# Register addresses of eight loaded offsets worked out at the load, three to an instruction, in a graph attention + MoE kernel

## What is computed

```python
h = jnp.einsum('ni,hid->nhd', layernorm(x), W)            # 4 heads of 64
e = (h[src] * a_src).sum(-1) + (h[dst] * a_dst).sum(-1)   # a score for each edge and head
e = jnp.where(e > 0, e, 0.2 * e)
alpha = jnp.exp(jnp.minimum(e - segment_max(e, dst)[dst], 20.0))
alpha = alpha / (segment_sum(alpha, dst)[dst] + 1e-08)
x = x + segment_sum(alpha[:, :, None] * h[src], dst).reshape(N, 256) @ W_out
t = layernorm(x)
probs = softmax(t @ router_w.T); rw, re = top_k(probs, 2); rw = rw / rw.sum(-1)
x = x + t + sum(combine[:, e] * (gelu(t @ w1[e] + b1[e]) @ w2[e] + b2[e]) for e in range(8))
```

## Time and profile before

| | before |
|---|---|
| median of three runs | 1516.63 us |
| time of the profiled execution | 1515.7 us |
| its span, first to last instruction | 1513.6 us |
| mean granted TensorE clock | 0.953 |
| TensorE matmuls busy | 1381.5 us (91%) |
| VectorE, ScalarE, GpSimd busy | 1108.2 (73%), 985.0 (65%), 840.0 us (55%) |

### The profile page before, as it was taken

The page is one execution under the profiler, slowest core; times in us unless marked ns, Lnnn a source line. Parts: engine busy times, 40 slices in busy tenths (PEclk is TensorE's granted clock), DMA queues, the critical chain, the costliest instruction groups (busy, mean ns, idle before and its releaser), DMA issues.

```text
span 1513.6 us, 28779 instructions
## 1 busy us (share of the span) xinstructions
PE 1381.5 (91%) x7177; PEld 1120.8 (74%) x7177; DVE 1108.2 (73%) x3057; ACT 985.0 (65%) x2522; POOL 840.0 (55%) x886
## 2 busy tenths in 40 slices
PE   5925775899999999999999999999999999999998
PEld 4723443688888888788878787878787878787887
DVE  6726775778787878787878787878777878777543
ACT  3713664567777767676767676767676767777732
POOL 1347777666666666666666665656565656661000
PEclk9965786699999999999999999999999999999999
DMA  9564654434444444444444444444444343464000
GB/s 223 145 196 121 191 148 118 134 102 122 112 122 113 121 113 120 115 118 118 120 113 120 116 114 119 117 118 111 123 109 128 104 132 99 134 89 66 1 18 18
DMA packets 89817, 174.79 MB, mean 115 GB/s; under 512 B 22471, under 2 KB 56081, under 8 KB 89625
## 3 DMA queue, kind: packets, MB, share of 16 engines
q0 software_dynamic: 40448, 111.89, 29.5%
q1 hardware_dynamic: 48103, 60.78, 13.2%
q10 hardware_dynamic: 1106, 0.27, 0.1%
HBM read 159.26 MB, written 14.43 MB: 115 GB/s over the span
## 4 chain that ended last, share of the span: by engine, by line
PE 65%; issue 8%; ACT 7%; DVE 6%; POOL 5%; ACTq 2%; DMA 1%; DVEq 0%; POOLq 0%
PE agg_ps L1148 22%; PE ob L1223 17%; PE hb L1177 14%; POOL ring L747 5%; PE kbank L1110 3%; PE ob L1259 3%; DVE ring L855 2%; ACT acc L1377 2%; PE ob L1229 2%; ACT agg_ps L1380 2%; ACTq L660 1%; PE kbank L1125 1%; ACT L1391 1%; PE kbank L1124 1%; ACT hT L1409 1%
## 5 line engine op out<-in xcount | busy, mean ns | idle before, releaser
L747 POOL DMA_INDIRECT ring<-table,srcE x832 | 808.0, 971 | 476.6 <-PE agg_ps L1148 237.5
L1148 PE MATMUL agg_ps<-ring,oh 128*128 128x260 f32 x1664 | 552.5, 425 | 19.1 <-ACT agg_ps L1380 15.7
L1377 ACT COPY acc<-agg_ps x831 | 306.7, 369 | 182.4 <-PE agg_ps L1148 109.4
L1223 PE MATMUL ob<-w_sb,hT 128*125 128x256 f32 x1600 | 408.7, 381 | 1.7
L1380 ACT COPY agg_ps<-zc 128x260 f32 x832 | 314.7, 378 | 98.7 <-ACT acc L1377 3.2
L1148 PEld LDWEIGHTS agg_ps<-ring,oh 128*128 128x128 f32 x1664 | 291.7, 199 | 79.6 <-issue 41.8
L1223 PEld LDWEIGHTS ob<-w_sb,hT 128*125 128x125 f32 x1600 | 295.8, 188 | 53.1 <-issue 9.2
L855 DVE TENSOR_TENSOR ring<-ring,kbank 128x1024 f32<-128x1024 f32 x208 | 244.9, 1215 | 51.9 <-ACT ring L1399 51.5
L1409 ACT ACTIVATE hT<-hb,b_sb 128x375 f32<-128x375 f32 (+1 forms) x272 | 153.7, 565 | 122.8 <-PE hb L1177 121.9
L992 DVE SCALAR_TENSOR_TENSOR y<-ob,cmb,y 125x256 f32<-125x256 f32 x400 | 189.2, 476 | 45.1 <-PE ob L1223 41.7
L1177 PE MATMUL hb<-xTh,w1l 128*128 128x376 f32 (+1 forms) x544 | 186.7, 424 | 0.0
(11 more groups left out here) (280 smaller groups left out, 1340.6 us busy)
## 6 DMA issues: line engine op xcount, KB each, us to landing
OT<-relb_d SPq DMA_DIRECT2D x52, 512.0 KB
ring<-table,srcE POOLq DMA_INDIRECT x832
y<-in_x_dram SPq DMA_DIRECT2D x50, 125.0 KB
out_dram<-y SPq DMA_DIRECT2D x50, 125.0 KB
table<-hrow SPq DMA_DIRECT2D x25, 227.5 KB
acc<-in_x_dram SPq DMA_DIRECT2D x2, 1568.0 KB
acc<-in_L_ffn_w_dram SPq DMA_DIRECT2D x1, 2048.0 KB, 11.9
w_sb<-in_L_ffn_w_dram SPq DMA_DIRECT2D x1, 2048.0 KB, 11.8
```

Of the source, the lines that this page charges most:

```text
L747: pool.indirect_dma_start(out=rings[b % RING][:, k, :], out_offset=None, in_=table[:, :], in_offset=bass.IndirectOffsetOnAxis(ap=srcE[:, t ...
L1148: T.matmul(aggf[:, bass.ds(bank_of[k // 8][k % 8], ROW)], oh[:, (4 * b + q) % OHQ, k % 4, :], rings[b % RING][:, k, :], start=False, stop= ...
L1223: t = T.matmul(o[0:Q, 0:D], hT[:, e % 2, f, cols], w2_sb[:, e, f, :], start=f == 0, stop=f == KC - 1)
L1377: A.copy(accf[:, bass.ds(row_of[h][k % 8], ROW)], aggf[:, bass.ds(closed[h][k % 8], ROW)]).then_inc(S["ev"], 1)
```

## The change

A new helper `worked_out(eng, views)` asks for the addresses of a list of views of one engine. It is called right behind each `loads` that brings table offsets, with the eight views that will be used (one on VectorE), and the matmuls and copies take the finished views. The compiler puts the work for eight addresses into three register instructions. Nothing else is edited, and the matmuls, copies and loads of TensorE and ScalarE keep their order.

```diff
--- before.py
+++ after.py
@@ -660,6 +660,10 @@
                 return nc.values_load_multi_w_load_instructions(ap, engines=[eng], min_val=0, max_val=top_,
                                                                 skip_runtime_bounds_check_because=WHY)[1]
 
+            def worked_out(eng, views):
+                for a in views:
+                    eng.lower_ap(a)
+
             FETCHED = 16 * 4
             fetched = lambda b: FETCHED * (b // RING + 1)
             HC = lambda g, e, f: 2 * NE * g + 2 * e + f + 1
@@ -838,13 +842,15 @@
                     first = {}
 
                     def bank_of_first(b):
-                        first["at"] = loads(ENG.DVE, tabs[0:1, b % 3, 0, 0:4], (AB - 1) * 512)[0]
+                        at = loads(ENG.DVE, tabs[0:1, b % 3, 0, 0:4], (AB - 1) * 512)[0]
+                        first["at"] = aggf[:, bass.ds(at, ROW)].rearrange("p (h w) -> p h w", h=H)
+                        worked_out(v, [first["at"]])
 
                     def rescale(b):
                         dve.wait_ge(S["sc"], b + 1)
                         dve.wait_ge(S["agg"], BT * b)
                         dve.wait_ge(S["zr"], BT * b - 1)
-                        a = aggf[:, bass.ds(first["at"], ROW)].rearrange("p (h w) -> p h w", h=H)
+                        a = first["at"]
                         v.tensor_tensor(a, a, sc[:, :].unsqueeze(2).to_broadcast([P, H, HW]), ALU.mult).then_inc(S["rs"], 1)
 
                     def message(b, q):
@@ -1097,7 +1103,9 @@
                     def blocks_of_tiles(b, half):
 
                         pe.wait_ge(fld[b % RING], fetched(b))
-                        block_of[half] = loads(ENG.PE, tabs[0:1, b % 3, 2, 8 * half:8 * half + 8], (NB - 1) * 3 * H)
+                        rows_ = loads(ENG.PE, tabs[0:1, b % 3, 2, 8 * half:8 * half + 8], (NB - 1) * 3 * H)
+                        block_of[half] = [d3[:, bass.ds(r, 3 * H)] for r in rows_]
+                        worked_out(T, block_of[half])
 
                     def d_of_edges(b, half):
                         if half == 0:
@@ -1107,7 +1115,7 @@
                                 pe.wait_ge(S["otc"], 1)
                         for j in range(8):
                             t = 8 * half + j
-                            m = T.matmul(D_ps[:, t * 3 * H:(t + 1) * 3 * H], OT[:, t * P:(t + 1) * P], d3[:, bass.ds(block_of[half][j], 3 * H)],
+                            m = T.matmul(D_ps[:, t * 3 * H:(t + 1) * 3 * H], OT[:, t * P:(t + 1) * P], block_of[half][j],
                                          start=True, stop=True)
                         if half == 1:
                             m.then_inc(S["D"], 1)
@@ -1130,7 +1138,9 @@
                     def banks_of_tiles(b, h):
 
                         pe.wait_ge(fld[b % RING], fetched(b))
-                        bank_of[h] = loads(ENG.PE, tabs[0:1, b % 3, 0, 8 * h:8 * h + 8], (AB - 1) * 512)
+                        at = loads(ENG.PE, tabs[0:1, b % 3, 0, 8 * h:8 * h + 8], (AB - 1) * 512)
+                        bank_of[h] = [aggf[:, bass.ds(r, ROW)] for r in at]
+                        worked_out(T, bank_of[h])
 
                     def aggregate(b, k):
                         t, q = b * BT + k, k // 4
@@ -1145,7 +1155,7 @@
                             pe.wait_ge(S["am"], 1)
                         elif t > 1:
                             pe.wait_ge(S["zr"], t - 1)
-                        T.matmul(aggf[:, bass.ds(bank_of[k // 8][k % 8], ROW)], oh[:, (4 * b + q) % OHQ, k % 4, :], rings[b % RING][:, k, :],
+                        T.matmul(bank_of[k // 8][k % 8], oh[:, (4 * b + q) % OHQ, k % 4, :], rings[b % RING][:, k, :],
                                  start=False, stop=True, skip_group_check=True).then_inc(S["agg"], 1)
 
                     def ahead(it, k):
@@ -1359,11 +1369,17 @@
                         if k == 11:
                             act.wait_ge(fld[b % RING], fetched(b))
                         if k in (5, 11):
-                            row_of[h] = loads(ENG.Activation, tabs[0:1, b % 3, 3, part], (NB - 1) * ROW)
+                            at = loads(ENG.Activation, tabs[0:1, b % 3, 3, part], (NB - 1) * ROW)
+                            row_of[h] = [accf[:, bass.ds(r, ROW)] for r in at]
+                            worked_out(A, row_of[h])
                         elif k in (3, 13):
-                            coming[h] = loads(ENG.Activation, tabs[0:1, b % 3, 1, part], (AB - 1) * 512)
+                            at = loads(ENG.Activation, tabs[0:1, b % 3, 1, part], (AB - 1) * 512)
+                            coming[h] = [aggf[:, bass.ds(r, ROW)] for r in at]
+                            worked_out(A, coming[h])
                         elif k in (7, 15):
-                            closed[h] = loads(ENG.Activation, tabs[0:1, b % 3, 4, part], (AB - 1) * 512)
+                            at = loads(ENG.Activation, tabs[0:1, b % 3, 4, part], (AB - 1) * 512)
+                            closed[h] = [aggf[:, bass.ds(r, ROW)] for r in at]
+                            worked_out(A, closed[h])
 
                     def evacuate(b, k):
 
@@ -1374,10 +1390,10 @@
                             act.wait_ge(S["agg"], t)
                             if t > 1:
                                 act.wait_ge(S["ev"], t - 1)
-                            A.copy(accf[:, bass.ds(row_of[h][k % 8], ROW)], aggf[:, bass.ds(closed[h][k % 8], ROW)]).then_inc(S["ev"], 1)
+                            A.copy(row_of[h][k % 8], closed[h][k % 8]).then_inc(S["ev"], 1)
                             act.wait_ge(S["ev"], t)
                             act.wait_ge(S["zr"], t)
-                        A.copy(aggf[:, bass.ds(coming[h][k % 8], ROW)], zc[:, 0:1].to_broadcast([P, ROW])).then_inc(S["zr"], 1)
+                        A.copy(coming[h][k % 8], zc[:, 0:1].to_broadcast([P, ROW])).then_inc(S["zr"], 1)
 
                     def evacuate_last():
                         act.wait_ge(S["agg"], NTS)
```

## The result

| | before | after |
|---|---|---|
| median | 1516.72 us (4 runs, 1516.58 to 1517.98) | 1478.93 us (4 runs, 1478.28 to 1479.79) |
| ratio | | 0.9749, 95% interval 0.9733 to 0.9766 |
| time of the profiled execution, and its span | 1515.7, 1513.6 us | 1478.9, 1476.0 us |
| mean granted TensorE clock | 0.953 | 0.955 |

The change saves 37.8 us. The forecast was 1482, the range 1467 to 1503.

The account below looks back on a forecast made before the run. TensorE, busy 196.5 of 200 us, was taken to set the pace. Savings of 35.5 and 2 us less 1 and 3 given back make 33.5, so 1515.7 becomes 1482.2, forecast 1482, range 1467 to 1503.

Parts of the forecast that it names:

- Score matmuls: TensorE's 16 score matmuls a batch: without register instructions between them, 35.5 us saved, between 29.5 and 39 us.
- Waits behind which an address stood: TensorE's aggregations that wait for a bank's clearing, 25 times: 0.08 us less each, 2 us saved, between nothing and 3.
- Three instructions behind each load: TensorE's 208 loads: 0.4 us more of sequencer each, mostly hidden by queued matmuls; 1 us lost at loads with less cover.
- ScalarE, put at nothing: ScalarE's two copies of a tile and its loads: relieved by some 60 us, but nothing of that shortens the kernel by itself.
- What grows back: TensorE's waits for ScalarE and VectorE grow as batches get shorter: 3 us given back, between none and 15.7.
- A register-addressed matmul that is itself slow for the sequencer: Rival, score matmuls: the register address itself slows the matmul, so only 29 us are saved, 1490 us; chance 0.14.
- The engine that takes back what TensorE saves: Rival: waits for VectorE's bursts and ScalarE's table loads take half of TensorE's saved time, 17 us left, 1499; chance 0.17.
- The slower rival: Rival: ScalarE's longer loads, 1.8 us a batch, reach TensorE through the clearing; at 60% the kernel takes 1538 us; chance 0.07.

Follow-up runs that it names:

- Scores alone: Only the addresses of the 16 score matmuls of a batch worked out at their loads, the rest as in the kernel before: 1493.31 against 1516.53 us, ratio 0.9853.

## Why the prediction was right

The time was within 3.1 us of the forecast, but two of its terms were wrong by 10 us and more, in opposite directions.

1. *Score matmuls, 35.5 us.* Right. The groups of eight fell from 62.1 to 25.4 us, 36.7 us; "both groups should take what the shortest one takes" is what the timeline shows (0.20 and 0.21 us). The busy time of the line fell by 29.3 us, near the lower bound of 29.5 that the prediction took from it: idle gaps of a starved group aren't in it.
2. *Waits behind which an address stood, 2 us.* Mis-sized: four aggregations and the transposes of xn are 16 us nearer to what stands before them. The price of one instruction was not the error: where the aggregation waits, its least distance behind the end of the clearing fell from 130 to 52 ns, 0.08 us as predicted. The count was: the prediction counted the 25 waits that the view of waits shows as idle, and an aggregation that is held up while the matmul before it still counts as busy isn't among them. ScalarE's share of it failed by the next point.
3. *Three instructions behind each load.* They take 74, 74 and 60 ns on TensorE, estimated at 61, and start 133 ns apart; from the end of the load to the end of the third it is 0.39 us, predicted 0.4. Nearly all are hidden, as said: from batch 4 on the next matmul of the program starts at least 0.77 us behind a load's end. The 1 us put down for the others is about what shows: behind the last load of batches 1, 2 and 3 tile 15's aggregation starts 0.44 us after the load's end, where it was 0.19. Even with the cover taken away a group lost only 0.26 us. That the waits now stand at the matmuls adds nothing to this cover. In the changed kernel none of the 203 loads of batches 0 to 51 starts before the end of the clearing that the aggregation ahead of it waits for. The closest 12 start 50 or 51 ns behind that end, some of them up to 1.5 us ahead of the aggregation itself. Before, the closest started 152 ns behind it. So the wait still holds a load that stands behind it; only the address instruction behind the wait is gone. That the sequencer "passes" the wait for `oh` at a score group is shown by no run. The term of the score matmuls doesn't need it: the groups take 0.20 and 0.21 us once their first matmul has started.
4. *ScalarE, put at nothing.* This step failed. "Nothing of that shortens the kernel by itself" was argued from ScalarE's waits for TensorE, 74 us. But these are a sum over all tiles; at k = 15, 12 and 6 it is TensorE that waits for ScalarE. In the kernel before, the aggregation stands there at its least distance behind the end of the clearing two tiles back (130 ns, within 5; 236 ns at k = 12, which also waits for `oh`) in 30, 15 and 12 of 45 batches. The two banks of lead are used up in these, and each clearing that comes 0.08 us sooner lets the aggregation two tiles on go sooner. Alone it is worth 10.3 us (1506.24). The idle time by its own issue grew as predicted in kind, from 0.44 us a time to 0.56 (99.9 us, 179 times), predicted 0.7, and cost nothing.
5. *What grows back, 3 us.* Mis-sized: 14.4 us. Of these 7.0 are the transpose of cmb, 4.0 that of eC and 3.4 the expert output. Scores alone bring back 10.4 of it. Ahead of the two transposes it is waits for VectorE, whose chains have a length of their own: where TensorE arrives sooner it waits. For the expert output no wait for VectorE of that size shows; its weight loads stand idle by their own issue for 11.6 us instead of 8.8, and the cause is open. The prediction took these from the sum of the waits of before, which says nothing of how close the others were behind.

Steps 2, 4 and 5 nearly cancel, 16 against 14.4, where the sum had 2 against 3 and 1. So the forecast's 1482 owes its nearness in part to chance. The lower bound of the range needed ScalarE's relief, and that came.

*The rivals.* A register-addressed matmul that is itself slow for the sequencer is refuted: eight of them without an instruction between take 0.20 us, each starting 25 ns behind the one before (median of 728 distances in the trace of the changed kernel). The engine that takes back what TensorE saves was partly true: 14.4 us, not half of the gain. ScalarE's table loads, which that rival names, are 101 of 1.28 us each before and after. On the slower chip the larger part of the gain is missing, but what took it isn't shown. The slower rival is refuted by the kernel with ScalarE's edit alone, which is faster.

## What to carry to other kernels

In this kernel an address from a register cost TensorE's sequencer some 0.12 us with its short matmul. Between short matmuls it showed: 36.7 us over 102 groups of eight. Between matmuls of 0.4 us next to nothing did: beside the other two parts, taking the 832 of the aggregation away was worth 1.2 us in the account. So look for runs of short instructions, not for the line with most instructions. Get all addresses of such a run out of it; whether they stand at the load or right ahead of the run, joined or single, made no difference here. A wait summed over all tiles in one direction (ScalarE for TensorE) doesn't mean that the other direction is slack: sort distances between starts by the place in the loop before an edit is put at nothing.

## What the runs showed of the hardware

- In the trace of the kernel before, the sequencers' rows hold one register instruction for each matmul or copy with such an offset: 832 for the score matmuls and 832 for the aggregations (37 ns each), 831 for the closing copies (55 ns) and 832 for the clearings (43 ns). Taken in order, each of these 1664 matmuls has its first weight load at least 48 ns behind the end of its own, and each of the 1663 copies starts at least 41 ns behind it. They also keep the waits: of the 830 aggregations that wait for a clearing, none has its register instruction start before the end of that clearing, and the closest starts 37 ns behind it.
- An instruction that works out three addresses takes 74 ns, on TensorE and on ScalarE (medians); one with two of TensorE's takes 60, one with one 37. In a row they start 133 ns apart on TensorE and 101 ns on ScalarE, so one with three takes hardly longer than the 0.12 us of a single one with its matmul.
- A single address instruction between two dependent copies of ScalarE lengthens the time between them from 0.032 to 0.114 us, 82 ns, where its own row says 43 ns.
- TensorE's sequencer runs ahead even past a load of 0.59 us: load and three instructions directly ahead of eight short matmuls delayed them by 0.26 us of about 1.
- A wait that stands at a matmul held the load behind it as well: in the changed kernel 0 of 203 loads of TensorE start before it is met, the closest 50 ns behind.
- Two chips gave the same durations of ScalarE's and VectorE's instructions and times 11% apart, 1516 and 1683 us. On the slower one the count that a score matmul raises rose 0.7 to 7.3 us behind the matmul's modelled end in 46 of 52 batches, on the other 13 to 15 ns behind it. Why stays open.
